# Windowed attention on one core: the third piece of q ahead of the attention, slabs measured in the first two pairs, a reordered prologue

## The reference, cut to what matters

```python
x = x + conv_preact(_gn(x))            # x: (16, 56, 56, 384) float32

def _gn(v):                            # group norm, 32 groups of 12 channels, over a whole image
    return (g - mean) / sqrt(var + 1e-5)

def conv_preact(x):                    # shifted-window attention
    x = roll(x, (-3, -3), axis=(1, 2))
    q, k, v = split(x @ w_qkv.T, 3)    # 12 heads of 32, windows of 7x7 = 49 tokens, 64 windows an image
    dots = q k^T * 32 ** -0.5 + pos_emb[rel] (+ shift masks in the last row and column of windows)
    out = softmax(dots) v
    out = out @ w_out.T + b_out
    return roll(out, (3, 3), axis=(1, 2))
```

## Time and profile before

| | value |
|---|---|
| median of the runs | 4250.94 us |
| the profiled execution | 4250.67 us |
| its span, first to last instruction | 4248.9 us |
| PE busy | 3998.8 us (94%) |
| DVE busy | 3676.0 us (87%) |
| ACT busy | 2313.5 us (54%) |
| POOL busy | 2102.1 us (49%) |
| chain that ended last | PE 81%, DVE 9%, ACT 6% |
| granted TensorE clock, mean | 0.996 |

### The profile page before, as it was taken

How to read it: one execution, slowest core, us unless ns; L and a number is a source line. 1 busy time by engine, 2 the same in 40 slices (tenths; PEclk the granted TensorE clock), 3 DMA queues, 4 the chain that set the end, 5 groups by cost and what they waited for, 6 DMA issues and landing times.

```text
span 4248.9 us, 163876 instructions
## 1 busy us (share of the span) xinstructions
PE 3998.8 (94%) x64304; PEld 2757.0 (65%) x64304; DVE 3676.0 (87%) x9291; ACT 2313.5 (54%) x4609; POOL 2102.1 (49%) x1813
## 2 busy tenths in 40 slices
PE   3999999999999999999999999999999999999998
PEld 1666666666666666666666666666666666666665
DVE  6888888888888888888888888888888888888886
ACT  0555555555555555555555555555555555555554
POOL 1445545544554545554455455545545455554554
PEclk9999999999999999999999999999999999999998
DMA  4445455454544554554454554545555545544542
GB/s 125 121 130 144 125 135 143 126 135 131 135 134 132 133 136 128 133 142 122 130 147 125 133 139 128 138 132 132 133 132 137 136 126 135 137 127 130 135 112 80
DMA packets 288056, 555.95 MB, mean 131 GB/s; under 512 B 45793, under 2 KB 197858, under 8 KB 279906
## 3 DMA queue, kind: packets, MB, share of 16 engines
q1 hardware_dynamic: 287298, 545.46, 48.5%
HBM read 237.00 MB, written 77.07 MB: 74 GB/s over the span
## 4 chain that ended last, share of the span: by engine, by line
PE 81%; DVE 9%; ACT 6%; issue 2%; SPq 1%; DMA 0%; POOL 0%; DVEq 0%; ACTq 0%; POOLq 0%
PE ps_pj L1205 23%; PE ps_pj L1201 16%; PE ps_post L1310 14%; PE ps_post L1292 5%; ACT ph L775 4%; PE ps_st L1269 4%; PE ps_sa L1239 3%; PE ps_st L1239 3%; PE ps_pv L1285 3%; PE ps_pv L1284 3%; PE ps_pv L1283 3%; PE ps_pj L1189 2%; ACT qk L686 2%; DVE qk L973 1%; DVE mx L1024 1%
## 5 line engine op out<-in xcount | busy, mean ns | idle before, releaser
L653 POOL TENSOR_TENSOR rb<-tq,cst 128x588 bf16<-128x588 bf16 x512 | 606.4, 1184 | 1851.7 <-ACT tq L762 1851.7
L686 ACT ACTIVATE qk<-ps_pj 128x392 f16<-128x392 f32 x768 | 382.0, 497 | 922.0 <-PE ps_pj L1205 915.8
L1205 PE MATMUL ps_pj<-xh,wh 128*128 128x392 f16 x2304 | 766.9, 333 | 116.5 <-DVE qk L973 105.3
L973 DVE TENSOR_TENSOR qk<-ps_pj,qk 128x392 f16<-128x392 f32 x768 | 434.0, 565 | 395.1 <-ACT qk L686 382.7
L775 ACT ACTIVATE ph<-ps_st,sc 64x588 f16<-64x588 f32 x1024 | 772.2, 754 | 6.4
L1205 PE MATMUL ps_pj<-xh,wl 128*128 128x392 f16 x2304 | 765.3, 332 | 0.0
L1205 PE MATMUL ps_pj<-xl,wh 128*128 128x392 f16 x2304 | 765.1, 332 | 0.0
L639 POOL TENSOR_TENSOR pl<-pf,ph 64x588 f16<-64x588 f32 x512 | 650.4, 1270 | 152.0 <-POOL rb L653 147.5
L1069 DVE TENSOR_TENSOR pl<-pf,ph 64x588 f16<-64x588 f32 x512 | 547.9, 1070 | 1.0 <-ACT ph L775 0.9
L1283 PE MATMUL ps_pv<-vh,ph 128*128 128x33 f16 x6144 | 516.6, 177 | 0.2 <-DVE pl L1069 0.2
L1285 PE MATMUL ps_pv<-vh,pl 128*128 128x33 f16 x6144 | 515.6, 177 | 0.0
(11 more groups left out here) (115 smaller groups left out, 8536.2 us busy)
## 6 DMA issues: line engine op xcount, KB each, us to landing
stack<-qk SPq DMA_DIRECT2D x1536, 147.0 KB
sx<-in_x SPq DMA_DIRECT2D x66, 1176.0 KB, 8.1
xb<-in_x SPq DMA_DIRECT2D x368, 192.0 KB
out<-xb SPq DMA_DIRECT2D x368, 192.0 KB
xs<-in_x SPq DMA_DIRECT2D x384, 84.0 KB
xs<-in_x SPq DMA_DIRECT2D x384, 63.0 KB
xs<-in_x SPq DMA_DIRECT2D x128, 66.0 KB
xs<-in_x SPq DMA_DIRECT2D x128, 49.5 KB
```

The costliest lines, as they stand in the source:

```text
L653: nc.gpsimd.tensor_tensor(rb[:, :, :, :], tq[:, :, :].unsqueeze(2).broadcast_to([128, 2, HH, N]), const_of("own_head").unsqueeze(1).unsque ...
L686: nc.scalar.activation(qk[:, K_HIGH if kind == "k" else Q_HIGH, i, :], ps_pj[bank][:, 0:RT], ACT.Copy).then_inc(s_hi, 1)
L973: nc.vector.tensor_tensor(qk[:, lp, i, :], ps_pj[bank][:, 0:RT], qk[:, hp, i, :], ALU.subtract).then_inc(s_pjr, 1)
L1205: m = mm(ps_pj[bank][:, 0:RT].rearrange("p (w n) -> p w n", w=NW), wa[:, c, o:o + 128], xa[:, b, c, :, 0:N], **on)
```

## The change

- In `FILL`, unit q2 (the third piece of q) moves in k = 1 and 5 from the second place, behind `attend` and `shift_rows`, to the first, right behind k1. `x0` stays second. PE, ACT and DVE all follow `FILL`.
- `ROW_UNITS`, the order of the very first row's units, was the order of `FILL`; now it is a list of its own, in which k2 stands before x0.
- `BN_SPREAD` goes from 7, 3, 1, 5 groups in the four pairs of a row to 8, 8, 0, 0; `BN_EARLY` from 11, 8, 5, 8 to 14, 12, 3, 3.
- SP's loads: slab 0, weights, slab 1, output weights, constants, bias. The 14 loads of the position table are issued by ACT.
- DVE measures slabs 0 and 1 before it looks at the weights.
- The transposed weights use six PSUM banks (`weight_bank`); ACT casts the high half, DVE only makes the low one.
- Slab 0 of image 1 is measured behind the first three `x_norm`, not ahead of them.

```diff
-        ([("k", 1)], [("q", 2), ("x", 0)], [("k", 2), ("x", 1)]),
+        ([("k", 1), ("q", 2)], [("x", 0)], [("k", 2), ("x", 1)]),
...
-ROW_UNITS = [u for parts in FILL for part in parts for u in part]
+ROW_UNITS = [("q", 0), ("k", 0), ("q", 1), ("k", 1), ("q", 2), ("k", 2), ("x", 0), ("v", 0), ("x", 1), ("v", 1), ("x", 2),
+             ("v", 2), ("v", 3)]
...
-BS_MADE, SC_MADE = 13, 17
+SCALES_MADE, BS_MADE, SC_MADE = 6, 13, 17
-BN_SPREAD, BN_EARLY = [7, 3, 1, 5, 7, 3, 1, 5], [11, 8, 5, 8, 0, 0, 0, 0]
+BN_SPREAD, BN_EARLY = [8, 8, 0, 0, 8, 8, 0, 0], [14, 12, 3, 3, 0, 0, 0, 0]
...
+        def weight_bank(u):
+            return (ps_pj[0], ps_pj[1], ps_post, ps_pv, ps_st[:, 0, :], ps_st[:, 1, :])[u % 6]
...
 # sync
-            sp.dma_start(cst[:, :], const[:, :]).then_inc(s_const, 16)
-            sp.dma_start(wnat[:, :, :], w_qkv.rearrange("(a p) c -> p a c", p=128)).then_inc(s_const, 16)
-            sp.dma_start(wonat[:, :, :], w_out.rearrange("(a p) c -> p a c", p=128)).then_inc(s_const, 16)
-            sp.dma_start(brow[:, :], b_out.rearrange("(a c) -> a c", a=1)).then_inc(s_const, 16)
             slab(0, 0, 0)
+            sp.dma_start(wnat[:, :, :], w_qkv.rearrange("(a p) c -> p a c", p=128)).then_inc(s_const, 16)
             slab(0, 1, 1)
-            sp.wait_ge(s_init, 1)
-            for r in range(WS):
-                ...
-                    sp.dma_start(bn[q:q + WS, :].rearrange("p (r c) -> p r c", r=WS), windows).then_inc(s_const, 16)
+            sp.dma_start(wonat[:, :, :], w_out.rearrange("(a p) c -> p a c", p=128)).then_inc(s_const, 16)
+            sp.dma_start(cst[:, :], const[:, :]).then_inc(s_const, 16)
+            sp.dma_start(brow[:, :], b_out.rearrange("(a c) -> a c", a=1)).then_inc(s_const, 16)
...
 # scalar
+            act.wait_ge(s_init, 1)
+            for r in range(WS):
+                ...
+                    act.dma_start(bn[q:q + WS, :].rearrange("p (r c) -> p r c", r=WS), windows).then_inc(s_const, 16)
+            act.wait_ge(s_pre, SCALES_MADE)
+            ...
+                        act.wait_ge(s_pj, u + 1)
+                        nc.scalar.activation(hi_[:, c, a * C:(a + 1) * C], weight_bank(u)[:, 0:C], ACT.Copy,
+                                             scale=s).then_inc(s_cast, 1)
...
 # vector
-            dve.wait_ge(s_slab[0], 16)
-            measure(0, range(GROUPS), True)
+            for s in range(2):
+                dve.wait_ge(s_slab[s], 16)
+                measure(s, range(GROUPS), True, s)
...
-                        dve.wait_ge(s_pj, u + 1)
-                        nc.vector.tensor_scalar(hi_[:, c, cols], ps_pj[u % 2][:, 0:C], s, None, ALU.mult).then_inc(s_cast, 1)
                         dve.wait_ge(s_cast, u + 1)
-                        nc.vector.scalar_tensor_tensor(lo_[:, c, cols], ps_pj[u % 2][:, 0:C], s, hi_[:, c, cols],
+                        nc.vector.scalar_tensor_tensor(lo_[:, c, cols], weight_bank(u)[:, 0:C], s, hi_[:, c, cols],
                                                        ALU.mult, ALU.subtract).then_inc(s_pjr, 1)
...
-            for s in range(1, SLABS):
+            for s in range(2, SLABS):
...
-            dve.wait_ge(s_slab[0], 16 * 3)
-            measure(0, range(GROUPS), True)
             dve.wait_ge(s_fz, FZ)
...
             for c in range(KC):
                 x_norm(u + 1, u % 2, c, c, 0, c)
                 u += 1
+            dve.wait_ge(s_slab[0], 16 * 3)
+            measure(0, range(GROUPS), True)
...
 # tensor
-                        bank_free(u + 1)
+                        need(pe, s_pjr, u + 1 - 6)
-                            m = nc.tensor.transpose(ps_pj[u % 2][:, i * 128:(i + 1) * 128], src[:, c * 128:(c + 1) * 128], ident)
+                            m = nc.tensor.transpose(weight_bank(u)[:, i * 128:(i + 1) * 128], src[:, c * 128:(c + 1) * 128], ident)
```

More of the change, by code:

```diff
@@ L499, in _ @@
             slab(0, 0, 0)
+            sp.dma_start(wnat[:, :, :], w_qkv.rearrange("(a p) c -> p a c", p=128)).then_inc(s_const, 16)
             slab(0, 1, 1)
-            sp.wait_ge(s_init, 1)
-            row = 2 * WS - 1
-            for r in range(WS):
-                windows = bass.AP(pos.tensor, r * row, [[1, WS], [row, WS], [1, WS]])
-                for at in (0, 64):
-                    q = at + r * WS
-                    sp.dma_start(bn[q:q + WS, :].rearrange("p (r c) -> p r c", r=WS), windows).then_inc(s_const, 16)
+            sp.dma_start(wonat[:, :, :], w_out.rearrange("(a p) c -> p a c", p=128)).then_inc(s_const, 16)
+            sp.dma_start(cst[:, :], const[:, :]).then_inc(s_const, 16)
+            sp.dma_start(brow[:, :], b_out.rearrange("(a c) -> a c", a=1)).then_inc(s_const, 16)
             def load_row(tk, odd):
@@ L677, in _ @@
         def _(act):
+            act.wait_ge(s_init, 1)
+            row = 2 * WS - 1
+            for r in range(WS):
+                windows = bass.AP(pos.tensor, r * row, [[1, WS], [row, WS], [1, WS]])
+                for at in (0, 64):
+                    q = at + r * WS
+                    act.dma_start(bn[q:q + WS, :].rearrange("p (r c) -> p r c", r=WS), windows).then_inc(s_const, 16)
+            act.wait_ge(s_pre, SCALES_MADE)
+            u = 0
+            for kind in ("w", "o"):
+                for c in range(KC):
+                    for a in range(3 if kind == "w" else 1):
+                        hi_ = wh if kind == "w" else woh
+                        s = sg[:, 0:1] if kind == "w" else sg[:, 1:2]
+                        act.wait_ge(s_pj, u + 1)
+                        nc.scalar.activation(hi_[:, c, a * C:(a + 1) * C], weight_bank(u)[:, 0:C], ACT.Copy,
+                                             scale=s).then_inc(s_cast, 1)
+                        u += 1
             def high(unit, kind, i, b, p_free, stack_sem, stack_need, bank):
```

## The result

| | before | after |
|---|---|---|
| median of 11 runs each, taken side by side | 4250.86 us | 4239.46 us (4236.27 to 4241.04) |
| ratio, with its 95% interval | | 0.9973 (0.9964 to 0.9983) |
| the profiled execution, and its span | 4250.67, 4248.9 | 4238.54, 4236.6 |

The change makes the kernel faster by 11.4 us. The forecast was 4212, with a range from 4170 to 4238: the sign is right, the gain is less than a third of the 39 us that I summed, and the time lies 1.5 above the upper end of the range.

What follows compares the result with a forecast made beforehand. PE was taken as the engine to watch, waiting about once a row for DVE's `low`, with DVE only about 0.12 behind being the bound. Gains of 23.2 (prologue) and 16 us (steady part) gave 4212, range 4170 to 4238.

Steps and rivals of the forecast that it cites:

- Odd row of it: Odd row of the finishing tick: moving q2 removes DVE's 0.96 idle before it; 12 us gained over 15 ticks.
- The ordinary row: 90 rows outside finishing ticks and last image: PE's saved microsecond is mostly given back, 0.04 a row, 4 us gained.
- The even row: Even row of the finishing tick, twelve groups in k = 1: 0.5 lost in each of 15, 8 us (2 to 15).
- rival 1: Ordinary rows: DVE's `pl` runs free and PE keeps its saved wait; 4122 whole (chance 0.08), 4165 in part (0.08).
- Rival 2: k = 1 of ordinary rows: POOL's residual takes the port before DVE's `pl`, 1.0 a row lost; 4306, chance 0.10.
- The prologue: Work before the main loop: terms (a) to (f), following each other on DVE, sum to 23.2 us gained (14 to 25).
- (a): Prologue, constants and load order: slabs land earlier, so DVE starts `amax` sooner; 1.8 us gained (0 to 2.3).
- (b): Prologue, weights: 13.6 us become 11 steps, 5.9 us, ACT's high halves being done before; 7.7 gained (5 to 8).
- (c): Prologue, slabs: slab 1 measured in (a)'s shadow, slabs 2 and 3 loaded by then; 15.95 become 9.6, 6.4 us gained.
- (d): Prologue: measuring slab 0 of image 1, 4.8 us, goes behind `x_norm`, beside POOL's and PE's work; 4.7 us gained.
- (e): Prologue: ACT's table load of 1.28 leaves the path, being done already in (b); 1.3 us gained.
- (f): Prologue, first row: k2 no longer stands behind x0 and its wait, so it and the first stack come 1.3 us earlier.

Runs made afterwards that it cites:

- e1: The kernel before with only q2 moved in FILL, old groups (three in k = 1) and old prologue: 4162.9 us, 0.9793.
- e2: The changed kernel with q2 put back in second place and the old groups, so the new prologue alone: 4230.21 us, 0.9954.
- e9: The changed kernel with only the small statistics steps moved away from where POOL is busy: 4201.68 us, 0.9883.
- e4: The changed kernel with BN_SPREAD groups 8, 3, 3, 2, three in k = 1 instead of eight: 4157.12 us, 0.9778.
- e3: The changed kernel with BN_SPREAD groups 8, 2, 3, 3, two in k = 1 instead of eight: 4147.38 us, 0.9756.
- e6: e3 with the small statistics steps moved to among the maxima in k = 6 and 7 and to the next tick's k = 0: 4117.38 us, 0.9685.
- e10: The kernel before with only the small statistics steps moved as in e6: 4240.24 us, 0.9973.
- e8: e6 with the finishing tick's groups (BN_EARLY) at 14, 2, 8, 8 instead of 14, 12, 3, 3: 4104.86 us, 0.9656.

## Why the prediction was wrong

**The step that failed** is "Odd row of it: ... I take 0.8 x 15 = 12 us gained (0 to 15)". It came out as 1.18 a tick lost, 18 us in all, so this term is off by 30. The forecast missed by 27, since the other terms together gained 3 more than I had summed. The mechanism that I named did work: k = 4 and 5 together went from 19.50 to 18.62, 0.9 gained. What I had not followed was what the row does next. The statistics steps, which I only named ("with statistics between all steps"), have no term in my sum: what they might meet on POOL in k = 6 and 7 I put at nothing, without a reason. The view of lines of the kernel before had two of them at 401 and 375 ns in the mean, twice what they take alone, and that was the sign of a collision already there (times | busy, mean ns | idle before).

```profile
L927 DVE SCALAR_TENSOR_TENSOR rs<-rs,varb 128x32 f32<-128x32 f32 x42 | 16.8, 401 | 1.0
```

With PE on time, POOL comes 0.23 nearer, the first step falls behind its `pl`, and k = 6 takes 9.03 in the mean. Shown by the two timelines above, by e1 (the same 1.27, with q2 alone moved), by e2 (gone with q2 put back), and by e9 (38 us back with only these steps moved).

**k = 7.** That PE, once left idle for 1.6 to 1.7 us, goes on at half its clock was in no term. It is 0.96 a tick in the mean, 14 of the 30 us; k = 6's 1.10 a tick is the rest, 16. That it follows the collision is shown by e9, where k = 7 is 7.31 and the clock falls in 2 of the ticks only, at k = 5. Why it falls in 9 ticks and not in all 15 is open; the tick that met no collision is among the six without.

**The ordinary row** gained 0.04 as forecast, 0.03 in the mean over all 88. The last image gained 8.6 for 8. The even row cost 0.16 for 0.5: DVE's `pl` ran free (0.75) in 14 of 15 ticks, the case for which I had 0.2, and took 1.53 in one.

**The range.** Its inner bounds, 4196 to 4236, don't follow from the bounds of the terms. In the order prologue, ordinary rows, even rows, odd rows and last image these add up to 25 + 4 - 2 + 15 + 8 = 50 and 14 + 4 - 15 + 0 + 8 = 11 us gained, so 4201 to 4240. That the measured 4239.46 lies within those is luck: the odd row's loss of 18 is far outside its own bounds, 0 to 15 gained.

**"The five more groups cost nothing here: with three, `pl` would be ready at 2121.25 and still meet POOL's"** was wrong, and it is the costliest sentence for whoever would act on it, though it did not touch the forecast of this kernel. The five groups cost 82 us against e4. I had computed that start at 0.03 behind POOL's, and took the order of two numbers 0.03 apart for certain. It belonged among the rivals: rival 1 (4165 or 4122) is what e1, e3 and e4 are, and its condition, "or DVE is ready before it", is met with three groups instead of eight.

**Rival 2**, the residual taking the port, did not occur in ordinary rows: `pl` was ready 0.58 before the residual (2137.91 against 2138.49).

**The prologue** gave 21.5 for 23.2. (a) was -1.1 and not +1.8. Slab 1 landed at 19.0: by my own reckoning the loads went at 0.23 MB a microsecond (4.09 MB) and not at 0.3, and PE's first transposition waited for the constants until 23.26. The Trainium skill, "DMA: Bandwidth & Descriptors", section "Queues, rings and completion order", has each DMA engine go round the queue rows packet by packet, and by it I had the small loads of ACT's queue land early. The trace has packets of both queues side by side from 3.1 on, but early the small loads were only in part: all were issued by 8.6, their last packet ended at 20.15, and the last packet of the constants, on SP's queue, at 22.64. So SP's queue came last, though the view of waits names `bn`, which shares a semaphore with the constants. (b) 5.8 for 5.9, (c) 9.6 for 9.6, (d) with (e) 5.8 for 6.0, all right. Behind q0 2.6 more were gained, against the 1.3 of (f); what made the difference was not followed up. The first `shift_rows` of the nine kernels with this prologue lies between 90.86 and 92.68, so a microsecond there is within what they differ by.

## What to carry to other kernels

Where two engines share a port, look for pairs of instructions that start within some 0.2 us of each other, and treat their order as open in both directions: a delay of 0.15 us on one of them is worth a microsecond, and so is a microsecond won elsewhere that shifts them. When a wait of the main engine goes, ask for each engine that follows it which instruction it now meets, in every kind of row and not only in the ordinary one. Small instructions whose mean is twice their shortest are the place to look at first; they can be moved to where the other engine is idle, which here was worth 30 and 38 us with q2 moved (e6, e9) and 10 without (e10).

## What the hardware showed that I had not expected

- The edge. By the profile's starts, DVE's `pl` still goes first when it is 0.03 or 0.04 behind POOL's (e1, e4), and no longer at 0.09 (four rows of e4, 0.09 to 0.11). The small step of the root goes first at 0.09 ahead (one tick of before) and no longer at 0.03 to 0.05 behind (after). So two starts within 0.1 of each other don't tell who has the port; the durations do. The loser then ends 0.62 after POOL if it is a `pl` of 0.76, and 0.04 after it if it is a step of 0.18, so all but some 0.14 of it waits. The other way round, POOL's `pl` of 1.27 ends 1.12 after DVE's (2203.57 to 2204.69 in e1), also all but 0.15.
- An instruction over 32 columns waits as long as a large one: 0.18 became 1.27.
- The wait for the port counts as busy: DVE's busy time is 3703.6 us in after and 3626.0 in e8, with the same 9279 instructions.
- PE's clock fell to half for 3.4 us at a time in the midst of the densest loop, in 9 of 14 cases behind a pause of 1.57 to 1.7 us. In the prologue of after it was at half from 31 to 68 us, where before it was at 1.00 until 110.
